# Layer 3's own attention: the place of the feature turns in a slot, and the numbering of the slots

## The reference

```
paths = sigmoid(x @ Wp + bp)                    # 8 heads, depth 5
agree = pq * pk + (1.0 - pq) * (1.0 - pk)
sim = cumprod(agree, axis=-1).sum(axis=-1) / DEPTH
sim = where(mask, -inf, sim)                    # causal
attn = softmax(sim)
V = (x @ Wv).reshape(Bx, Tx, H, DH)
ctx = einsum('bhqk,bhkd->bhqd', attn, V)
return ctx @ Wo                                 # x is the layer norm of the stream
```

## Time and profile before

| what | value |
|---|---|
| median of three runs | 2256.19 us |
| lowest and highest of the three | 2253.4 and 2260.17 us |
| the profiled execution | 2252.15 us |
| its span, first to last instruction | 2250.3 us |
| mean granted clock of TensorE | 0.872 of full |
| this stage (1909.5 to 1972.9 us of the span) | 63.4 us |
| granted clock in this stage | 0.87 |

### The profile page before, as it was taken

One profiled execution on the slowest core, in us unless ns is written; L12 is line 12 of the kernel. 1 busy time (PEld: TensorE's weight loads), 2 busy tenths in 40 slices (PEclk: granted clock), 3 DMA queues, 4 the chain that ended last, 5 costly groups with the idle time before them and its releaser, 6 DMA issues.

```text
span 2250.3 us, 57628 instructions
## 1 busy us (share of the span) xinstructions
PE 1991.1 (88%) x22720; PEld 1449.0 (64%) x22720; DVE 1335.2 (59%) x3559; ACT 904.6 (40%) x3432; POOL 562.6 (25%) x1360
## 2 busy tenths in 40 slices
PE   7999999889987998998978788998999999789844
PEld 4899998777566665567866655665654545556623
DVE  6676766765355787545636615886262220678787
ACT  2455554543155664302334523664211111246522
POOL 3566665222011000102335502331000000411111
PEclk9655555999999998999999989999999999889955
DMA  3000001004000001100030000000030000000000
GB/s 135 4 5 5 5 5 43 40 1 187 0 5 8 9 12 70 72 0 24 1 134 5 2 1 8 12 9 2 10 146 0 1 0 4 1 12 14 3 0 17
DMA packets 8025, 56.94 MB, mean 25 GB/s; under 512 B 792, under 2 KB 5248, under 8 KB 5984
## 3 DMA queue, kind: packets, MB, share of 16 engines
q1 hardware_dynamic: 7760, 53.27, 6.1%
HBM read 52.35 MB, written 0.92 MB: 24 GB/s over the span
## 4 chain that ended last, share of the span: by engine, by line
PE 68%; DVE 14%; ACT 7%; issue 6%; POOL 4%; DMA 1%; POOLq 0%; DVEq 0%; SPq 0%; ACTq 0%
PE banks L269 44%; PE banks L274 8%; PE banks L1390 6%; PE banks L963 3%; ACT memory L1011 2%; PE banks L989 2%; DVE memory L1492 2%; PE banks L1543 1%; ACT memory L1417 1%; POOL memory L1449 1%; ACT memory L1424 1%; DVE memory L1498 1%; DVE memory L1273 1%; ACT memory L1256 1%; DVE memory L1501 1%
## 5 line engine op out<-in xcount | busy, mean ns | idle before, releaser
L269 PE MATMUL banks<-memory 128*112 128x256 f32 (+7 forms) x4192 | 1121.4, 423 | 100.7 <-DVE memory L3549 21.5
L269 PEld LDWEIGHTS banks<-memory 128*128 128x128 f32 (+2 forms) x4192 | 699.2, 194 | 431.5 <-issue 276.2
L274 PE MATMUL banks<-memory 112*125 112x112 f32 (+3 forms) x2000 | 301.9, 283 | 76.3 <-DVE memory L850 26.8
L274 PEld LDWEIGHTS banks<-memory 112*125 112x125 f32 (+3 forms) x2000 | 235.9, 171 | 190.3 <-issue 99.8
L1390 PE MATMUL banks<-memory 128*128 128x8 bf16 (+2 forms) x10752 | 306.8, 175 | 14.2 <-DVE memory L1475 1.4
L1390 PEld LDWEIGHTS banks<-memory 128*128 128x128 bf16 x10752 | 295.7, 104 | 25.9 <-POOL memory L1449 23.8
L1011 ACT ACTIVATE memory<-banks,memory 112x375 f32<-112x375 f32 x384 | 215.0, 577 | 25.4 <-DVE memory L1049 25.1
L1049 DVE TENSOR_REDUCE memory<-banks 112x2 f32<-112x750 f32 x192 | 171.0, 933 | 37.3 <-PE banks L963 37.0
L1492 DVE TENSOR_REDUCE memory<-banks 128x48 f32<-128x192 f32 x448 | 121.8, 291 | 62.0 <-PE banks L1390 47.7
L1057 DVE COPY memory<-banks 125x448 f32<-125x448 f32 x192 | 116.8, 618 | 10.7 <-PE banks L274 6.2
L963 PE MATMUL banks<-memory 32*112 32x375 f32 x768 | 88.5, 530 | 19.6 <-ACT memory L1011 17.4
(11 more groups left out here) (240 smaller groups left out, 2436.5 us busy)
## 6 DMA issues: line engine op xcount, KB each, us to landing
memory<-in_l2x SPq DMA_DIRECT2D x1, 7680.0 KB, 21.4
memory<-in_l2f SPq DMA_DIRECT2D x1, 7168.0 KB, 19.4
memory<-in_l1f SPq DMA_DIRECT2D x1, 4617.0 KB, 14.5
memory<-in_ctxT SPq DMA_DIRECT2D x24, 187.5 KB
memory<-in_l2f SPq DMA_DIRECT2D x1, 4096.0 KB, 12.2
memory<-in_l3f SPq DMA_DIRECT2D x1, 3073.0 KB, 22.0
memory<-in_l2a SPq DMA_DIRECT2D x1, 3072.0 KB, 19.5
memory<-in_l0f SPq DMA_DIRECT2D x1, 2304.0 KB, 9.3
```

Source lines behind the costliest of these rows:

```text
L269: ins = self.nc.tensor.matmul(out, weights[i], acts[i], start=i == 0, stop=i == n - 1)
L274: return self.nc.tensor.transpose(out, in_, self.ident[0:n, 0:n])
```

## The change

The table of steps is put into another order, with other lags, and the loop over slots runs over B + 4 in place of B + 5. The steps themselves, their buffers and their waits are left as they are.

```
--- before.py
+++ after.py
@@ -2522,8 +2522,8 @@
 
 
 
-    SLOT = (("y", 5), ("values", 4), ("divide", 4), ("scores", 3), ("stats", 0), ("feats", 2), ("mask", 3), ("paths", 1),
-            ("xn", 0), ("v", 1), ("features", 1), ("xT", 0))
+    SLOT = (("xT", 0), ("y", 4), ("values", 3), ("divide", 3), ("scores", 2), ("stats", -1), ("paths", 0), ("mask", 2),
+            ("xn", -1), ("v", 0), ("features", 0), ("feats", 1))
     H, F = 8, 2 ** DEPTH
 
     def __init__(self, k):
@@ -2542,7 +2542,7 @@
         self.ring = (4, 5, 7)
 
     def order(self):
-        for n in range(B + 5):
+        for n in range(B + 4):
             for step, lag in self.SLOT:
                 if (step in ("stats", "xn")) <= n - lag < B:
                     yield step, n - lag
```

## The result

The changed kernel takes 2262.39 us (median of 11 runs, 2259.5 to 2265.81) against 2256.19 before (11 runs, 2251.64 to 2260.17). The ratio on record is 1.0032, 95% interval 1.0024 to 1.0041; it is drawn from all runs of both kernels and is not the quotient of the two medians, which is 1.0027. So the change is 0.3% slower, just about at the bound up to which I called it no change. The forecast was 2257.1 us with a range to 2263.6; the time is inside, 5.3 us above the likeliest. What I worked out was 0.9 us, what came was 6.2, so most of it is not in my sum.

What follows compares the result with a forecast made beforehand. It took a loop through TensorE, VectorE and GpSimd to set the 7.22 us slot. Terms 0 + 0.72 + 0.17 gave +0.9 us on the 2256.19 median, so 2257.1 us, range 2250.9 to 2263.6.

Steps and rivals of the forecast that it cites:

- The reading of the edit: Whole stage: VectorE and GpSimd orders unchanged, thirteen against twelve slots only counting; feats moves behind paths and v on TensorE.
- rival A: Slot loop: one slot less saves a steady slot's time, 7.22 us, giving 2249.0 us, 0.32% faster; chance 0.04.
- Term 1: Steady slot on TensorE: moving feats costs 0, since the same pieces precede the same 2.41 us gap.
- Term 2: Ring of banks: y(0) to y(3) each wait for VectorE's copy of v, 4 x 0.18 = 0.72 us slower.
- Term 3: First slots: later feats(0) delays the copy of xT(2), the exponential's table load and turn xT(3), 0.17 us slower.
- Rival B: First slots: y's wait is hidden and earlier paths(1) and v(1) carry through, 0.6 us less, 2255.6; chance 0.12.
- rival D: Whole stage: new short waits keep TensorE at its lower clock, up to 11.0 us more, 2267.2, 0.49% slower; chance 0.05.

Runs made afterwards that it cites:

- b_head: The kernel before, with TensorE's first turn of the stage also waiting for VectorE's first statistics; 2263.11 us against 2255.17, ratio 1.0039.

## Why the prediction was right and where it was not

**The reading of the edit** held. VectorE's and GpSimd's sequences are the same, thirteen against twelve slots gave nothing, and rival A is out.

**Term 1**, feats in the steady slot at nothing: right at a held clock, where both orders have slots of 7.22 us (with banks by kind). The gap was there with 2.38 us.

**Term 2**, y's wait, four times 0.18 us: right in mechanism, too large in its sum. From the turn to y's first matmul it went from 0.25 to 0.43 us for y(1), from 0.25 to 0.42 for y(2) and from 0.31 to 0.42 for y(3), but for y(0), which both kernels run at the lower clock, it was 0.43 before and after. That is 0.46 us for 0.72.

**Term 3**, 0.17 us in the first slots: feats(0) came at 5.28 us after the first turn, the number worked out, but the table load only 0.05 later and xT(3) 0.06 in place of 0.17. ScalarE was through with feats(0) 1.09 us after its turn and not 1.13, and its next copy overlapped that by 0.11 us and not 0.04. Rival B's gain did not come in the changed kernel.

**The step that failed** is the one against rival D: "the gaps stay where they were and as long, within 0.2 us". That was true, and it was no argument. The sum took its slots from one profile and treated their clocks, 1.00 here and 0.78 there, as given; they are outcomes of the timing, and 0.2 us was more than the kernel before had to spare at xT(5) and y(1). The whole form of D did not come, since the clock returned to 1.00 for parts of the stage. The small form of D, "one low stretch more or one fewer", was the right mechanism with too low a price: I gave 1.1 to 1.8 us, up to 2.5 with both, and the stage paid 6.4, since after the one fall the later low stretches also stood elsewhere: +0.9, +1.1, +2.4 in the next three and +1.9 in the tail. I had written 64.3 us for the stage at a like clock; by the same cut it was 69.7. That the time lies in the range is luck: the sum explains 0.9 us of it, and the range reached so far only because the scatter of the runs was in it.

What was shown in profiles, one of each kernel but for the two that were repeated: that of the loss 6.4 us lie in the stage and 1.4 behind it, twice over; that y's waits, the changed order without them (with banks by kind), a later head, or one wait of 0.13 us give the same fall at the same moment; that filling one gap undoes it. Only argued: why the moments stand where they do. Not explained: why the stages behind this one are 1.4 to 3.6 us longer in some of the kernels, and why one wait did not show in the whole time.

## What to carry to other kernels

Before an edit is costed at a few tenths, look at how the granted clock lies over the slots: where equal slots have clocks of 1.00 and 0.78, the time of a stage is a matter of margins, and two profiles of the same kernel show whether its pattern is fixed. A delay of TensorE behind an idle gap can then cost many times its own length, here 3.4 us for 0.13, and a null result in such a stage says little about the edit. Ask also which work stands in the low stretch: on the loop it costs time, in front of an idle gap it may cost none. If the idle gap can't be closed, matmuls that nobody needs, about as long as the gap, held the clock here and made the stage readable; then check what the later stages give back.

## What the runs showed of the hardware

The pattern of the clock was fixed to the work and not to the time since the start: the stage began at 1910.5, 1910.8, 1916.4 and 1918.1 us, and its first fall stood about 11.2 us after the first turn each time. Not every later piece repeated: from 38.5 to 41.9 us one profile of before has 1.00 and the other 0.50. In b_head, whose first turn was 1.12 us later, the first fall stood about 1.1 us nearer to that turn, so by that one profile it goes by something ahead of the stage. Six matmuls of 128x112 by 128x256 in fp32 took 2.75 us at 2.4 GHz in a gap of 2.4 us, and the steady slot was as long with them as without (7.22 us).
